# First attention: key weights multiplied into the queries, and scores taken against the tokens themselves

## The reference

```
q[h]      = x @ Wq[h]                       # 64 queries x 64 features
k[h]      = tokens @ Wk[h]                  # 128 keys x 64 features
content   = (q[h] + content_bias[h]) @ k[h].T
position  = rel_shift((q[h] + position_bias[h]) @ r[h].T)
probs     = softmax((content + position) / 8)
out      += probs @ tokens @ (Wv[h] @ Wo[h])
```

## Time and profile before

| | us |
|---|---|
| runs shown | 1948.61, 1948.49, 1951.13 (median 1948.61) |
| profiled execution: time | 1958.74 |
| profiled execution: span from first to last instruction | 1957.2 |
| first attention's last product on TensorE (L603) | starts at 619.04 |

### The profile page before, as it was taken

The page is one execution under the profiler, slowest core; times in us unless marked ns, Lnnn a source line. Parts: engine busy times, 40 slices in busy tenths (PEclk is TensorE's granted clock), DMA queues, the critical chain, the costliest instruction groups (busy, mean ns, idle before and its releaser), DMA issues. The chain is left out here.

```text
span 1957.2 us, 54686 instructions
## 1 busy us (share of the span) xinstructions
PE 1623.2 (83%) x17114; PEld 1297.1 (66%) x17114; DVE 1360.1 (69%) x4172; ACT 1171.2 (60%) x3299; POOL 944.9 (48%) x1373
## 2 busy tenths in 40 slices
PE   6899999999996969999998764379998895439992
PEld 6788888888884747767776641157776674437771
DVE  3777777777775648888776538868887774337873
ACT  2776777677764437778776322258887771127771
POOL 2354344444532445556664424434454444646773
PEclk8999999999998979999998877779999995559996
DMA  8866666766661022230000000000000000136665
GB/s 228 159 149 144 155 148 139 160 142 153 146 148 45 0 103 106 100 110 21 19 18 8 1 1 1 0 4 1 0 10 13 12 9 21 43 99 206 220 211 163
DMA packets 214820, 167.19 MB, mean 85 GB/s; under 512 B 27633, under 2 KB 188785, under 8 KB 214449
## 3 DMA queue, kind: packets, MB, share of 16 engines
q1 hardware_dynamic: 206128, 142.88, 29.3%
q0 software_dynamic: 8576, 22.88, 3.6%
HBM read 91.92 MB, written 73.76 MB: 85 GB/s over the span
## 5 line engine op out<-in xcount | busy, mean ns | idle before, releaser
L738 ACT ACTIVATE sb_probs<-sb_probs,sb_work 128x128 f32<-128x128 f32 x512 | 198.6, 405 | 117.4 <-DVE sb_work L641 117.4
L281 POOL TENSOR_SCALAR sb_next_var_eps<-sb_next_moments 128x1 f32<-128x1 f32 (+1 forms) x184 | 45.3, 246 | 422.3 <-DVE sb_next_moments L721 241.9
L890 POOL TENSOR_TENSOR sb_work<-sb_work,sb_cols 128x512 f32<-128x512 f32 x128 | 134.1, 1048 | 216.2 <-ACT sb_work L1107 134.2
L1033 DVE TENSOR_REDUCE sb_work<-PS 128x8 f32<-128x512 f32 x256 | 175.2, 684 | 46.6 <-PE PS L932 44.9
L1035 DVE TENSOR_TENSOR sb_work<-PS,sb_work 128x512 f32<-128x512 f32 x256 | 177.0, 691 | 8.8
L1067 ACT ACTIVATE sb_work<-sb_work 128x512 f32<-128x512 f32 x256 | 161.5, 631 | 32.8 <-DVE sb_work L1035 26.8
L906 PE MATMUL PS<-sb_ident,sb_work 128*128 128x128 f32 x1024 | 151.0, 288 | 15.4 <-ACT sb_work L1107 9.9
L959 PEld LDWEIGHTS PS<-sb_v_ones,sb_work 128*64 128x64 f32 x4096 | 133.0, 140 | 24.0 <-issue 15.8
L959 PE MATMUL PS<-sb_v_ones,sb_work 128*64 128x18 f32 x4096 | 144.9, 214 | 4.3 <-ACT sb_work L1073 2.8
L1073 ACT ACTIVATE sb_work<-PS 128x512 f32<-128x512 f32 x256 | 139.6, 595 | 10.3 <-PE PS L906 7.0
L906 PEld LDWEIGHTS PS<-sb_ident,sb_work 128*128 128x128 f32 x1024 | 115.0, 146 | 42.7 <-issue 30.5
(11 more groups left out here) (276 smaller groups left out, 4454.4 us busy)
## 6 DMA issues: line engine op xcount, KB each, us to landing
rel_scratch<-sb_work SPq DMA_DIRECT2D x64, 516.0 KB, 7.8
sb_work<-rel_scratch SPq DMA_DIRECT2D x64, 512.0 KB, 6.6
expert_rows<-sb_blank SPq DMA_DIRECT2D x36, 520.0 KB, 2.9
sb_w_up<-expert_halves SPq DMA_DIRECT2D x23, 512.0 KB
sb_w_down<-expert_halves SPq DMA_DIRECT2D x23, 512.0 KB
expert_halves<-sb_e_halves POOLq DMA_DIRECT2D x16, 512.0 KB, 6.1
sb_work<-expert_rows SPq DMA_DIRECT2D x23, 260.0 KB
sb_e_raw<-e_W POOLq DMA_DIRECT2D x16, 256.0 KB, 5.5
```

Source lines behind the costliest of these rows:

```text
L738: ins = e.activation(probs[:, j], probs[:, j], ACT.Exp, bias=neg_max[:, j:j + 1], scale=-1.0, accum_out=row_sum[:, j:j + 1])
L890: e.tensor_tensor(k_masked[:, u3], k_sb[:, u3].rearrange("p (b k) -> p b k", b=2).unsqueeze(2) .to_broadcast([P, 2, 4, S]), col("place").u ...
L1033: e.tensor_reduce(top, mine, AX.X, ALU.max).then_inc(sem("att_max_ready"), 1)
```

## The change

The keys are no longer projected. Instead each head's biased queries (the same `q0T`, in the same place) are multiplied with the head's key weights, 16 products per tile of 64 rows deep, 128 x 128, in float32, each head into a quarter of a bank; ScalarE copies the four banks to `q_over_k`. The scores are then products of this (stationary, 128 rows deep, the 64 query rows of a sequence) with the transposed tokens of the sequence (128 x 128). The transposed tokens are kept whole in `kvT`, in four buffers. `w_k0_hi`, `w_k0_lo`, `x_own`, `x_hi0`, `x_lo0` and what fills them are gone.

```
@@ buffers
-                ("w_k0_hi", [P, H * DK], F32R), ("w_k0_lo", [P, H * DK], F32R)
+                ("w_kT", [P, H // 2, D], F32), ("kvT", [P, 4, 2 * KL], F32)
-        k0T = carve((2, H // 2, 2 * KL), 0)
+        q_over_k = carve((2, 4, 4, P), 0)
-        x_own = carve((P,))
-        x_hi0, x_lo0 = (sb("x0_" + part, [P, 2 * KL], F32R) for part in ("hi", "lo"))
@@ l0_tensor, scores (after the same two waits)
-                    for ch in range(H // 2):
-                        i = ch % 4
-                        for hh in range(2):
-                            g, r = 2 * (ch // 4) + hh, slice(DK * hh, DK * hh + DK)
-                            if i == 0:
...
+                    for g in range(4):
...
+                        for i in range(4):
                             for b in range(2):
                                 ins = e.matmul(PS[S * b:S * b + S, 4 + g, i * KL:i * KL + KL],
-                                               q0T[r, v1, ch, S * b:S * b + S], k0T[r, v1, ch, KL * b:KL * b + KL],
+                                               q_over_k[:, v1, g, i, S * b:S * b + S],
+                                               kvT[:, (u + 1) % 4, KL * b:KL * b + KL],
                                                start=True, stop=True, skip_group_check=True)
-                            if i == 3:
-                                ins.then_inc(sem("l0_scores_done"), 1)
+                        ins.then_inc(sem("l0_scores_done"), 1)
@@ l0_tensor, queries
-                            ins = e.matmul(PS[:, 1 + half, i * P:i * P + P], w_q0[:, P * ch:P * ch + P], x_own,
+                            ins = e.matmul(PS[:, 1 + half, i * P:i * P + P].rearrange("p (b q) -> p b q", b=2),
+                                           w_q0[:, P * ch:P * ch + P],
+                                           kvT[:, (u + 3) % 4].rearrange("p (b a k) -> p a b k", b=2, a=2)[:, 1],
@@ l0_tensor, keys (the waits for banks 0 to 3 stay, at i == 0 of each g)
-                    for j in range(4):
...
-                        for i in range(2):
-                            at = P * (2 * j + i)
-                            ins = product_in_parts(e, PS[:, j, 2 * KL * i:2 * KL * i + 2 * KL],
-                                                   (w_k0_hi[:, at:at + P], w_k0_lo[:, at:at + P]),
-                                                   (x_hi0[:, :], x_lo0[:, :]))
-                        ins.then_inc(sem("l0_k_done"), 1)
+                    for half in range(2):
+                        for i in range(4):
+                            ch = 4 * half + i
+                            for hh in range(2):
+                                g, r = 2 * half + hh, slice(DK * hh, DK * hh + DK)
...
+                                ins = e.matmul(PS[:, g, i * P:i * P + P], w_kT[r, ch], q0T[r, v3, ch],
+                                               start=True, stop=True, skip_group_check=True)
+                                if i == 3:
+                                    ins.then_inc(sem("l0_k_done"), 1)
@@ l0_vector, once
-            e.wait_ge(sem("l0_qk_loaded"), 32)
-            e.tensor_copy(w_k0_hi[:, :], w_k0).then_inc(sem("l0_setup_kept"), 1)
-            e.wait_ge(sem("l0_setup_kept"), 2)
-            e.tensor_tensor(w_k0_lo[:, :], w_k0, w_k0_hi[:, :].bitcast(F32), ALU.subtract)\
-                .then_inc(sem("l0_setup_kept"), 1)
@@ l0_vector, transposed tokens
-                    e.tensor_copy(x_own.rearrange("p (b q) -> p b q", b=2),
-                                  transposed.rearrange("p (b a k) -> p a b k", b=2, a=2)[:, 1])
-                    e.tensor_copy(x_hi0[:, :], transposed).then_inc(sem("l0_kv_kept"), 1)
+                    e.tensor_copy(kvT[:, (u + 3) % 4], transposed).then_inc(sem("l0_kv_kept"), 1)
                     e.tensor_reduce(pooled[:, bass.ds(2 * t, 2)],
-                                    transposed.rearrange("p (b a k) -> p a b k", b=2, a=2)[:, 0], AX.X, ALU.add)
-                    e.wait_ge(sem("l0_kv_kept"), 2 * t + 1)
-                    e.tensor_tensor(x_lo0[:, :], transposed, x_hi0[:, :].bitcast(F32), ALU.subtract)\
+                                    transposed.rearrange("p (b a k) -> p a b k", b=2, a=2)[:, 0], AX.X, ALU.add)\
                         .then_inc(sem("l0_kv_kept"), 1)
@@ l0_scalar
-                        e.activation(k0T[:, v3, 2 * j:2 * j + 2], PS[:, j].rearrange("p (i k) -> p i k", i=2), ACT.Copy)\
+                        e.activation(q_over_k[:, v3, j], PS[:, j].rearrange("p (i q) -> p i q", i=4), ACT.Copy)\
                             .then_inc(sem("l0_k_kept"), 1)
@@ layout of the inputs
-    T["l0_Wq"], T["l0_Wk"] = L0["Wq"], L0["Wk"]
+    T["l0_Wq"], T["l0_WkT"] = L0["Wq"], c(L0["Wk"].reshape(D, H // 2, P).transpose(2, 1, 0))
```

More of the change, by code:

```diff
@@ L207, in build @@
         with ExitStack() as first:
-            VO, rel_bias, w_q0, w_k0_hi, w_k0_lo, rT, probs, probsT, pkvT = (
+            VO, rel_bias, w_q0, w_kT, kvT, rT, probs, probsT, pkvT = (
                 first.enter_context(nc.sbuf_tensor("sb_" + name, shape, dt))
                 for name, shape, dt in (("VO", [P, H, P], F32), ("rel_bias", [P, H, KL + 1], F32),
-                                        ("w_q0", [P, H * DK], F32), ("w_k0_hi", [P, H * DK], F32R),
-                                        ("w_k0_lo", [P, H * DK], F32R), ("rT", [P, H // 2, KL], F32),
+                                        ("w_q0", [P, H * DK], F32), ("w_kT", [P, H // 2, D], F32),
+                                        ("kvT", [P, 4, 2 * KL], F32), ("rT", [P, H // 2, KL], F32),
                                         ("probs", [P, H, KL], F32), ("probsT", [P, H, P], F32),
@@ L304, in build @@
         wvT, wo0 = probsT[0:DK], pkvT[0:DK]
-        w_k0 = probs[:, 0:H * DK // KL].rearrange("p j k -> p (j k)")
         wr = carve((H, DK), 2 * H * KL)
@@ L314, in build @@
                             (position_bias[:, :], a["l0_pb"])],
-                    "qk": [(w_k0, a["l0_Wk"]), (w_q0[:, :], a["l0_Wq"])],
+                    "qk": [(w_kT[:, :, :], a["l0_WkT"]), (w_q0[:, :], a["l0_Wq"])],
                     "vo": [(wvT, a["l0_WvT"]), (wo0, a["l0_Wo"])]}
@@ L504, in step @@
                     wait_alone(e, sem("l0_k_kept"), 4 * t + 4)
-                    for ch in range(H // 2):
-                        i = ch % 4
-                        for hh in range(2):
-                            g, r = 2 * (ch // 4) + hh, slice(DK * hh, DK * hh + DK)
-                            if i == 0:
[L510 to L513, removed]
+                    for g in range(4):
+                        if has(2):
+                            wait_alone(e, sem("l0_rel_kept"), 4 * (n + 2) + g + 1)
+                        else:
+                            wait_alone(e, sem("l0_rows_done"), 4 * n + g + 1)
+                        for i in range(4):
                             for b in range(2):
                                 ins = e.matmul(PS[S * b:S * b + S, 4 + g, i * KL:i * KL + KL],
-                                               q0T[r, v1, ch, S * b:S * b + S], k0T[r, v1, ch, KL * b:KL * b + KL],
+                                               q_over_k[:, v1, g, i, S * b:S * b + S],
+                                               kvT[:, (u + 1) % 4, KL * b:KL * b + KL],
                                                start=True, stop=True, skip_group_check=True)
-                            if i == 3:
-                                ins.then_inc(sem("l0_scores_done"), 1)
+                        ins.then_inc(sem("l0_scores_done"), 1)
                 if has(3):
@@ L576, in step @@
                     e.wait_ge(sem("l0_kv_kept"), 2 * t + 2)
-                    for j in range(4):
[L578 to L585, removed]
-                        for i in range(2):
-                            at = P * (2 * j + i)
-                            ins = product_in_parts(e, PS[:, j, 2 * KL * i:2 * KL * i + 2 * KL],
-                                                   (w_k0_hi[:, at:at + P], w_k0_lo[:, at:at + P]),
-                                                   (x_hi0[:, :], x_lo0[:, :]))
-                        ins.then_inc(sem("l0_k_done"), 1)
+                    for half in range(2):
[3 more added lines that the diff above has]
+                                g, r = 2 * half + hh, slice(DK * hh, DK * hh + DK)
+                                if i == 0:
+                                    if g == 0 and has(0):
+                                        e.wait_ge(sem("l0_pkvT_kept"), 4 * n + 4)
+                                    elif 1 <= g <= 2:
+                                        e.wait_ge(sem("l0_q_kept"), 2 * t + g)
+                                    elif g == 3 and has(0):
+                                        e.wait_ge(sem("l0_out_added"), n + 1)
+                                    elif g == 3 and has(2):
+                                        e.wait_ge(sem("l0_k_kept"), 4 * (n + 2) + 4)
```

(4 more changed lines are left out.)

## The result

| | before | after |
|---|---|---|
| median of runs, us | 1949.87 (1948.49 to 1956.75) | 2026.63 (2024.73 to 2027.06) |
| profiled execution, span | 1957.2 | 2024.6 |
| first attention's last product on TensorE starts at | 619.04 | 696.74 |

The ratio is 1.0382, 95% interval [1.0358, 1.0405]: slower, as forecast, but by 77 us where 39 were forecast, and outside the range. The first attention grew by 696.74 - 619.04 = 77.7 us; all of it is there. (The span grew less, 67.4, since the profiled execution of before had 10 us more behind this phase.)

The account below looks back on a forecast made before the run. TensorE's own work was taken to bound the first attention; +37.7 us for 29 steady steps, +3.6 after and -1.3 before them gave +40.0, forecast 1988 us. Its own range was 1975 to 1999, or 1970 to 2004 including the case without the gate.

Parts of the forecast that it names:

- What bounds the kernel: First attention: TensorE's own work sets the 17.86 us step; other engines matter only where they make it wait.
- The scores: TensorE's score products, now 128 rows deep, run as 32 pairs: slot 1.91 to 3.71 us, +1.80 a step.
- Exposed loads: Rival: the new scores' weight loads do not overlap, a pair takes 0.152 us; 2024 us in total, chance 0.08.
- no pairing: Rival: the scores' two column halves run one after another, 3.7 us more a step; 2103 us, chance 0.03.
- The rule that the prediction weighed: Trainium skill: a weight load overlaps running matmuls only when its row group differs; the new scores' loads would be exposed.
- The keys' place: New products replace the keys on TensorE, but transposes wait for ScalarE's copies: scores start at 4.30, not 4.79; 0.50 saved.
- "inside the other" wait: Transposes' group 2 wants the probabilities at 2.87, ready at 3.05 us; this wait was held to lie within the copies' 0.5.
- 0.1 at the start of the keys' stage: ScalarE's copies of the new products were to begin 1.1 us after the stage's start, against 1.00 before.
- The sum: First attention: +1.30 us for each of 29 steady steps, +3.6 after them, -1.3 before them, +40.0 in all.
- at the end (forecast 3.6): After the steady steps, two more score stages without a keys' stage: 2 x 1.80 = +3.6 us.
- the lead-in: Before the steady steps, where VectorE bounds: shorter keys' stages and a shorter token step give back 1.3 us.

Follow-up runs that it names:

- e12: e9 with VectorE's second normalisation put ahead of the third and fourth position-score groups; 1973.49 us, 1.0086 against the kernel before.
- e9: The changed kernel, loop kept, with 64 more TensorE instructions (repeated score products) ahead of the loop; 1991.57 us, 1.0160 against the kernel before.
- e1: The changed kernel with TensorE's steps of the first attention written out, without the loop; 1989.25 us, 1.0182 against the kernel before.
- e11: The kernel before, loop untouched, with 264 more TensorE instructions (repeated score products) ahead of the loop; ratio 0.9985.
- e5: The kernel before, loop kept, with each of four products of 512 columns (probabilities times tokens) cut into two of 256; ratio 1.0125.
- e7: The kernel before, loop kept, with two of the four products of 512 columns cut into two; ratio 1.0141.
- e8: The changed kernel, loop kept, with 4 of the 16 output products of each tile left out; 1989.62 us, 1.0169 against the kernel before.
- e10: The kernel before, loop untouched, with 66 more TensorE instructions (repeated score products) ahead of the loop; ratio 1.0154.
- e3: The kernel before with TensorE's steps of the first attention written out, without the loop; ratio 1.0002.

## Why the prediction was right or wrong

1. *What bounds the kernel*: right in the main. TensorE's own work set the step before and sets it after, but for a wait of 0.33 a step (point 3) and the loop's returns (point 5).
2. *The scores*: right. Forecast slot 3.71, measured 3.65, 0.114 a pair, the pace of L515's groups of four. The two halves of the array work at once at 128 rows, and their loads are hidden. Exposed loads and no pairing are both refuted, the first although its 2024 came near the measured time: a pair takes 0.114 and not 0.152. A total that fits is no evidence for its mechanism. The rule that the prediction weighed there does not hold for this shape.
3. *The keys' place*: the amount right by luck (4.30 forecast, 4.30 measured), the reason wrong. I took the 2.74 us of ScalarE's four copies as their own pace. They were paced by TensorE, which began a new bank every 0.71 us. Free of it they take less:

```profile
325.17 2.06 ACT L762 ACTIVATE sb_work<-PS 128x512 f32<-128x512 f32 x4 [0.99 <-PE PS L589]
```

   They are done 3.15 after the stage's start, not 3.84. The last of them is wanted only with the last group of transposes, in time even in e12, where nothing else holds these. VectorE's normalisation, which I had "inside the other" wait, is the one that is late:

```profile
323.39 2.48 DVE L651 TENSOR_TENSOR sb_work<-PS,sb_work 128x512 f32<-128x512 f32 x4 [0.69 <-PE PS L570]
...
326.02 1.23 DVE L645 TENSOR_TENSOR sb_probs<-sb_probs,sb_work 128x1024 f32<-128x1024 f32 x1
```

   It ends at 327.25, 3.17 after the stage's start, and the transposes go on at 327.39, with two groups still to do. VectorE's work hangs on L570's start, which the shorter stage behind it does not move.
4. *A smaller term*: 0.1 at the start of the keys' stage fell away; L570's slot in front of it is 1.89 (1.99 in the earlier trace rows), and the new products have its shape. With 1.74 for the scores in place of 1.80 the step is 18.99: +1.13 and not +1.30.
5. *The sum*: this failed. "A steady step: +1.80 - 0.50 = +1.30. There are 29" took all steps as alike, and so put the loop's five returns at nothing. Without the stalls the change costs 1.6 to 1.8% (e9, e1), 31 to 35 us, inside the forecast's own range. The returns cost 39 to 43 us more by the ratios. In the trace of after, from one return's L532 to the next and less four steps of 18.99, they cost 7.0 to 9.9 each, of which 4.5 to 7.3 is idle and the rest the lower clock. The 77.7 us of the two traces are 32.8 for 29 steps, 43.7 for the returns and 3.7 at the end (forecast 3.6), less 2.5 in the lead-in (forecast 1.3, but the lead-in moves by as much without the change: the steady steps begin at 62.71 in the kernel before and at 59.20 in e11, which has more to do there). No part of the prediction priced the instructions themselves: "24 records go, 32 come in" was read as time on the array, and not as 64 instructions more a round and code that begins later. Nor did I ask what the profile's line of instruction transfers would do.

The mechanism that the runs support: TensorE's instructions come in blocks, a loop that lies in seven of them is kept, and one that reaches into an eighth is fetched again at each return. The Trainium skill (page "Runtime: NRT & Kernel Launch", section "Instruction fetch mechanics") has part of it: instructions are refilled in blocks of 16 KiB, 256 instructions; TensorE holds 2048; and a taken branch stalls for the fetch when its target is not in a window of two blocks. The transfers of 16 KB here agree with the block, and the place of the second stops fits 256. The window of two blocks does not agree: the kernel before returns five times over 1637 recorded instructions, more than six blocks, without a transfer. The 2048 would be eight blocks, and by the table above no loop in eight is kept. That one of the eight is taken up by what comes next, as the nine transfers a return suggest (eight of the loop and one beyond), is my reading; no run separates it from a store of seven.

The edge also gives a reason why the changed kernel stands still twice a return. Its loop begins 28 instructions before it, so the first block that is fetched again would be used up at once, and TensorE would wait for the next (2.47 and 4.37 us; over the five returns 4.5 to 7.3 together). In e5, e7, e8 and e10 the edge is further off, and the second stop is short or missing (2.5 to 4.0 first, then at most 1.2).

## What to carry to other kernels

Price the instructions of a loop that runs on the device as well as their work: a body near the size that is kept can tip over by a few instructions inside it or ahead of it, and then each return costs 5 to 10 us here. Look for it in the profile as idle time ended by "issue" at the loop's start, and in the count of instruction transfers; write the loop out or shift it, and only then judge the change. And before a copy's pace is taken over into a forecast, see whether the copy was waiting for each piece.

## What the runs showed of the hardware that was not expected

A loop that is kept has no instruction transfers at all (none in 373 us of the kernel before); one that is not has nine a round (45 in the five returns of each kernel that stalls, all 104 against 59). Steps of 17.9 us written out are fetched without a stall (1.0002, e3). An idle of 3 us at the loop's return was followed by a stretch at 1.2 GHz: in e10 the granted clock was 0.50 from 283.00 to 286.60, and the scores behind it took 2.92 in place of 1.91.
